# Row maxima of two heads in the two halves of the array, start rows on two queues, routing and experts in an even chain

## The chip, the cores and the metric

The kernel runs on one core of one Trainium2 chip. The metric is the device time of one launch in microseconds (us). Of the kernel before there are three timed runs and one profiled execution.

## What is computed

One transformer layer over 1,024 tokens of width 256, in f32:

```
xn  = layernorm(x)
q, k, v = xn @ Wq.T, xn @ Wk.T, xn @ Wv.T            # 16 heads of 16 columns
scores  = q @ k.T / sqrt(16)                         # causal
std     = softmax(scores) @ v
gsa     = softmax(scores + sensitivity * splat(q, k)) @ v
attn    = ((1 - blend) * std + blend * gsa) @ Wo.T
moe     = two of 16 experts a token (top 2 of sqrt(softplus(xn @ gate.T)) + bias, 128 slots an expert), plus a shared expert
out     = x + attn + moe
```

`splat` is a product of 16 features a head (8 Gaussians, and the same 8 times a tanh) of the query and of the key.

## The kernel before

**Numbers.** The score products run in bf16. Each f32 factor is split in up to three bf16 parts (`split`, line 570 makes the first part, line 575 the second, line 368 on GpSimd and `third_of` on VectorE the third), and six products of parts are stacked along the contraction: `stage` tiles `qs` and `ks` hold for each head 6 x 16 = 96 rows (`RUNS`, `KR`), and two more rows (96 and 97) that subtract the row maximum, which comes as a pair of bf16 rows out of `mT` against rows of ones. `fq` and `fk` hold the same for the features. The rows are copied from `split` by DMA: 12 issues a group of two heads for `qs` and `ks` (`load_qk_row`, line 309), 18 for the features (`load_feature_row`, lines 316 and 322) and one for a correction that is zero here (line 325).

**Groups and slots.** The 16 heads are done two at a time, in 8 groups. A group is 6 pairs of key tiles (`PAIRS`), and a pair has 4 slots, so 24 slots a group. In a pair TensorE runs `std` (scores, line 788, masks line 791), `splat` (line 800, which adds onto the same PSUM banks), and `pv` (line 817: probabilities times v, four streams in the four 32-column strips of the array). ScalarE takes the exponential of each (line 636). Side work goes between them, by a table `PLAN[g][slot]` that all engines walk: on TensorE slot 0 stands between `pv` and the first `splat`, slot 1 between the two `splat`, slot 2 after them, slot 3 between the two `std`. The side work shares three PSUM banks (`AB`); a task waits until the one three places before it has been read (`aux_free`).

**Side work.** `max`/`max2`: the maxima of the next group's rows, plain scores (K = 96, lines 710 to 720) into one bank a head and block, read by VectorE (lines 1088 to 1093), 22 reads a group; `shift`: their transposition and 2 DMAs of 16 rows (line 444); `route` 0 to 7: the top two and the slots, VectorE only but for one product; `sgu`, `shT`, `sy`: the shared expert for one of 8 token tiles; `xT`, `gu`, `hT`, `y`: one of 16 experts (line 735, line 745 with tanh at line 641, line 749, line 754); `oT`, `rows`, `out`: the output; `add`: the gathered expert rows. The shared expert fills groups 0 and 1 (four tiles each), the experts groups 2 to 5 (four each, at slots 0, 2, 5, 6 and 5, 7, 9, 10 of each half group), routing is in slots 1 to 20 of group 0, the adds in groups 6 and 7.

**Before the groups.** `PRO` is the order of TensorE's prologue: transposes of xn, projections, parameters (`par`), features (`feat`, lines 687 to 690), router logits (`gate`, line 669), v (line 695). Then come the maxima of group 0 (`max0`, `PRE1` with 8 of the 16 of `max1`; the other 8 in slots 0 to 3 of group 0), and `std(0,0,0)`, which waits for the shift rows. SyncE issues nearly all transfers, in its program order: after the 24 `qs`/`ks` rows of groups 0 and 1 it reads a flag (`wide`: is a correction needed), branches, issues the 19 feature rows of group 0 with the shift rows among them, and goes on with the table.

Of the kernel before, what the change touches and what calls it, by code (L numbers as in the profile page):

```python
# [6 lines left out]
def bass_splat_attention_moe_layer(nc, x, wqkvo, positions, directions, log_scales, log_amplitudes,  # L7
# [5 lines left out]
    T, D = x.shape  # L13
# [20 lines left out]
    KS = KR + 2  # L34
    NEG = -1.0e30
# [12 lines left out]
    with ctx:  # L48
# [17 lines left out]
        stage = [sb(f"stage{n}", [KS, QB if n < 2 else 2, GH, T], bf16) for n in range(4)]  # L66
# [90 lines left out]
        aux_full, aux_free = sem("aux_full"), sem("aux_free")  # L157
        std_ready, std_exp, gsa_ready, gsa_exp = sem("std_ready"), sem("std_exp"), sem("gsa_ready"), sem("gsa_exp")
# [15 lines left out]
        own_step = sem("own_step")  # L174
# [6 lines left out]
        PRO += [("proj", (s, m, tc)) for m in range(KD) for s in range(2) for tc in range(NC)] + [("par", 0)]  # L181
        PRO += [("feat", (s, tc, w)) for s in range(2) for tc in range(NC) for w in range(2)]
        PRO += [("gate", 0)] + [("v", n) for n in range(NT // 2)]
# [31 lines left out]
        max0 = [("max2", (h,)) for h in range(GH)] + [("max", (h, it, 0)) for h in range(GH) for it in range(2, TC)]  # L215
        max1 = [("max", (h, it, pc)) for h in range(GH) for it in range(TC, NT) for pc in range(2)]
# [12 lines left out]
        SG = 4  # L229
        G0, G1 = 2, 6  # L230
        EG = E // (G1 - G0)


        def spread_late(tasks, first, last):
            late = [n for n in range(first, last + 1) if n % 4]
            return [(late[len(late) * n // len(tasks)], t) for n, t in enumerate(tasks)]
# [6 lines left out]
        def chain(tasks, at):  # L243
            return [(n + 12 * (f // 2), (k, at + f)) for f in range(4) for k, n in tasks[f % 2]]
        SHARED = ((("sgu", 2), ("shT", 5), ("sy", 6)), (("sgu", 7), ("shT", 9), ("sy", 10)))
        EXPERT = ((("xT", 0), ("gu", 2), ("hT", 5), ("y", 6)), (("xT", 5), ("gu", 7), ("hT", 9), ("y", 10)))
        PLAN = []
        for g in range(NG):
            lists = [[(11, ("oT", 0))]]
# [6 lines left out]
            if g == 0:  # L256
                lists.append(spread([("route", k) for k in range(ROUTE)], 1, 22))
            if g < G0:
                lists.append(chain(SHARED, g * SG))
            elif g < G1:  # L260
                lists.append(chain(EXPERT, (g - G0) * EG))
            if g == NG // 2:
                lists.append([(14, ("rows", (0, 0))), (18, ("rows", (0, 1)))])
            if g == NG - 2:
                lists.append(spread([("add", (k, n)) for n in range(TC) for k in range(2)], 12, 22))
            if g == NG - 1:
                lists.append(spread([("add", (k, n)) for n in range(TC, NT) for k in range(2)], 1, 12))
                lists.append([(6, ("out", (TC, 0))), (10, ("out", (TC + 2, 0))), (13, ("rows", (1, 0))),
                              (16, ("out", (0, 2))), (19, ("out", (2, 2)))])
# [21 lines left out]
        def group_of(kind, e):  # L291
            return e // SG if kind in ("sgu", "shT", "sy") else G0 + e // EG

        def count_of(kind, e):
            return place(group_of(kind, e), (kind, e))[1]
# [5 lines left out]
        N_QK, N_F = 12, 19  # L301

        def load_qk_row(eng, g, b, j, done):
            n, h = j // 6, j % 6 // 3
            row, part, num = RUNS[j % 3]
            head = g * GH + h
            m, p0 = head * HD // P, head * HD % P
            src = split[p0:p0 + HD, 0, part:part + 1, m, :].to_broadcast((HD, num, T)) if n == 0 else split[p0:p0 + HD, 1, 0:num, m, :]
            eng.dma_start(stage[n][row:row + num * HD, b, h, :], src).then_inc(done, 16)

        def load_feature_row(eng, g, b, j, done):
# [12 lines left out]
            else:  # L324
                eng.dma_start(fq[KR:KS, b, :, :], gap_d[g:g + 1, :, :, :].rearrange("o s h t -> (o s) h t")).then_inc(done, 16)

        @block.gpsimd
        def _(pool):
# [22 lines left out]
            pool.wait_ge(ones_set, 1)  # L351
# [918 lines left out]
```

## Time and profile before

| | us |
|---|---|
| median of 3 runs | 376.65 (376.22 to 376.99) |
| the profiled execution | 378.75 |
| its span in the trace | 376.9 |
| TensorE matmul busy | 334.7 (89%) |
| VectorE busy | 230.7 (61%) |
| ScalarE busy | 194.1 (51%) |
| GpSimd busy | 65.7 (17%) |
| granted TensorE clock, mean | 0.947 |

Times are us from the span's start. A granted clock of 1.00 is 2.4 GHz, 0.50 is 1.2 GHz. The chain that ended last is 72% TensorE, 14% VectorE, 9% ScalarE. By the first `std` of each group, the groups start at 64.64, 118.37, 155.61, 193.76, 231.92, 270.67, 308.82 and 335.34.

### The profile page before, as it was taken

The page shows a single profiled execution, that of the slowest core. Times are in us where ns is not written, and L with a number is a line of the kernel's source. Part 1 is how long each engine was busy: PE and PEld are TensorE (multiplying, and loading weights), DVE is VectorE, ACT ScalarE, POOL GpSimd, SP SyncE. Part 2 cuts the span into 40 slices and gives each one's busy share as a digit, 9 for nine tenths or more (in the row PEclk, how much of TensorE's full clock was granted, in tenths as well). Part 3 has the DMA queues.
Part 4 walks back from the last instruction along what each step waited for, and adds up shares of the span by engine and source line. Part 5 has one row for each costly group of instructions (what it writes and reads, how often), then busy time and mean ns, then how long its engine had stood idle before and what let it go on. Part 6 is the DMA issues. An engine that isn't in the chain of part 4 may idle for free.

```text
span 376.9 us, 6181 instructions
## 1 busy us (share of the span) xinstructions
PE 334.7 (89%) x2172; PEld 174.8 (46%) x2172; DVE 230.7 (61%) x614; ACT 194.1 (51%) x278; POOL 65.7 (17%) x82
## 2 busy tenths in 40 slices
PE   0999996788979999999999999999999999989965
PEld 0643663343345544554455445544554454335433
DVE  4555857587674665567556655766577558776222
ACT  1699824525414365436543654366346547767530
POOL 7200140400047530110111011102010007710000
PEclk9999768598979999999999999999999999999995
DMA  6408623304341354245655565547555525510011
GB/s 220 131 0 103 107 38 41 60 13 60 47 135 15 41 75 73 71 89 102 142 153 105 113 139 153 107 93 154 129 125 111 79 53 127 143 42 2 0 57 56
DMA packets 27330, 33.01 MB, mean 88 GB/s; under 512 B 6593, under 2 KB 20097, under 8 KB 27297
## 3 DMA queue, kind: packets, MB, share of 16 engines
q1 hardware_dynamic: 23745, 28.32, 37.4%
q0 software_dynamic: 2128, 4.22, 3.9%
q8 instruction: 19, 0.31, 0.4%
q10 hardware_dynamic: 1424, 0.04, 0.2%
q14 instruction: 14, 0.11, 0.1%
HBM read 15.60 MB, written 4.28 MB: 53 GB/s over the span
## 4 chain that ended last, share of the span: by engine, by line
PE 72%; DVE 14%; ACT 9%; issue 3%; DMA 1%; SPq 0%; DVEq 0%; ACTq 0%
PE ps L817 16%; PE ps L745 9%; PE ps L800 8%; PE ps L788 7%; PE ps L754 7%; PE ps L718 6%; ACT arena_p L636 6%; DVE mx L1093 5%; PE ps L676 4%; PE ps L773 2%; PE ps L695 2%; PE ps L758 2%; PE ps L791 2%; DMA acc<-in_x_dram 1%; ACT small L641 1%
## 5 line engine op out<-in xcount | busy, mean ns | idle before, releaser
L636 ACT ACTIVATE arena_p<-ps 128x1024 f32<-128x1024 f32 (+1 forms) x192 | 147.2, 811 | 79.4 <-PE ps L800 53.7
L1093 DVE TENSOR_REDUCE mx<-ps 128x1 f32<-128x512 f32 (+3 forms) x160 | 89.3, 590 | 33.2 <-PE ps L718 22.7
L817 PE MATMUL ps<-arena_p,v_full 128*32 128x512 f32 (+3 forms) x768 | 72.6, 496 | 0.6 <-ACT arena_p L636 0.6
L718 PE MATMUL ps<-stage 96*128 96x512 bf16 (+3 forms) x160 | 51.5, 362 | 7.1 <-DVE mx L1093 4.7
L788 PE MATMUL ps<-stage 98*128 98x512 bf16 (+1 forms) x192 | 51.9, 337 | 4.7 <-ACT arena_p L636 4.2
L800 PE MATMUL ps<-stage 98*128 98x512 bf16 (+1 forms) x192 | 47.4, 332 | 3.0 <-ACT arena_p L636 2.4
L641 ACT ACTIVATE small<-ps 128x176 f32<-128x176 f32 x24 | 7.6, 318 | 64.1 <-PE ps L745 64.1
L387 POOL DMA_INDIRECT wt<-xn_scratch,ids_sb x16 | 15.2, 951 | 133.2 <-PE ps L735 127.6
L817 PEld LDWEIGHTS ps<-arena_p,v_full 128*32 128x32 f32 x768 | 20.2, 110 | 35.4 <-issue 30.3
L754 PE MATMUL ps<-arena_o,small 88*128 88x256 f32 x96 | 27.4, 409 | 8.3 <-DVE small L1116 6.3
L788 PEld LDWEIGHTS ps<-stage 98*128 98x128 bf16 x192 | 18.8, 100 | 23.5 <-ACT arena_p L636 9.8
L718 PEld LDWEIGHTS ps<-stage 96*128 96x128 bf16 x160 | 15.3, 100 | 27.0 <-issue 11.2
L800 PEld LDWEIGHTS ps<-stage 98*128 98x128 bf16 x192 | 14.9, 98 | 26.8 <-ACT arena_p L636 13.5
L791 PE MATMUL ps<-mask_t,ident_b 128*128 128x128 bf16 x128 | 26.5, 225 | 0.0
L754 PEld LDWEIGHTS ps<-arena_o,small 88*128 88x128 f32 x96 | 16.7, 193 | 14.4 <-DVE small L1116 9.7
L745 PE MATMUL ps<-w_sb,wt 128*128 128x352 f32 x64 | 23.0, 482 | 0.1
L395 POOL DMA_INDIRECT ids_scratch<-tok,sidx x16 | 15.5, 968 | 42.0 <-DVE sidx L1047 37.5
L720 PE MATMUL ps<-mask_n,ident_b 128*128 128x128 bf16 x96 | 22.0, 229 | 0.0
L417 POOL DMA_INDIRECT xx<-ye_scratch,gidx x16 | 15.2, 948 | 35.2 <-issue 35.2
L1144 DVE COPY pv_sb<-ps 128x512 f32<-128x512 f32 x16 | 11.1, 692 | 14.6 <-PE ps L817 13.9
L1112 DVE SCALAR_TENSOR_TENSOR small<-small,ps 128x176 f32<-128x176 f32 x24 | 8.1, 338 | 18.1 <-ACT small L641 16.8
L916 DVE TENSOR_TENSOR acc<-ps,acc 128x256 f32<-128x256 f32 (+1 forms) x14 | 7.5, 538 | 18.3 <-PE ps L773 13.5
(193 smaller groups left out, 418.5 us busy)
## 6 DMA issues: line engine op xcount, KB each, us to landing
w_sb<-in_w_dram SPq DMA_DIRECT2D x16, 352.0 KB
stage<-split SPq DMA_DIRECT2D x48, 96.0 KB, 2.9
stage<-split SPq DMA_DIRECT2D x48, 64.0 KB, 2.7
arena_o<-in_w_dram SPq DMA_DIRECT2D x16, 176.0 KB
stage<-split SPq DMA_DIRECT2D x80, 32.0 KB, 2.5
ye_scratch<-wt SPq DMA_DIRECT2D x16, 128.0 KB, 1.8
stage<-split SPq DMA_DIRECT2D x32, 48.0 KB
acc<-in_x_dram SPq DMA_DIRECT2D x2, 512.0 KB, 4.6
```

The lines of the kernel that those rows point to most:

```text
L387: nc.gpsimd.indirect_dma_start(out=xe[:, e % XB, :], out_offset=None, in_=xn_d[:, :], in_offset=bass.IndirectOffsetOnAxis(ap=ids_sb[:, e:e ...
L395: nc.gpsimd.indirect_dma_start(out=ids_d[:, :], out_offset=bass.IndirectOffsetOnAxis(ap=sidx[:, k, n:n + 1], axis=0), in_=tok[:, n:n + 1], ...
L636: A(to, ps[:, 1 + 2 * s:3 + 2 * s, off:CH], ACT.Exp, scale=SCALE).then_inc(done, 1)
L718: ins = M(b[:, 0:n1 - n0], lhs, ks[0:KR, pr, h, n0:n1], start=True, stop=not diag)
L720: ins = M(b[:, n1 - n0 - P:n1 - n0], ident_b[:, :], mask_n[:, :], start=False, stop=True)
L745: ins = M(b[:, 0:2 * I], lhs, w13_sb[:, wb, k, :], start=k == 0, stop=k == KD - 1)
L754: ins = M(b[:, 0:D], hT[:, c, :], w2_sb[:, wb, c, :], start=c == 0, stop=c == 1)
L788: ins = M(b[:, off:CH], ks[:, pr, h, (jb + s) * P:(jb + s + 1) * P], qs[:, pr, h, ic * CH + off:(ic + 1) * CH], start=True, stop=not diag)
L791: ins = M(b[:, off:off + P], ident_b[:, :], mask_t[:, :], start=False, stop=True)
L800: ins = M(ps[:, 1 + 2 * s + h, off:CH], fk[:, pr, h, (jb + s) * P:(jb + s + 1) * P], fq[:, pr, h, ic * CH + off:(ic + 1) * CH], start=Fals ...
L817: ins = M(ps[c:c + 2 * HD, 0, off:CH], v_full[:, jb + s, g * GH + h, :], of, start=jb + s == 0, stop=end)
L1093: V.reduce_max(mx[:, it // TC, h, it % TC, pc:pc + 1], b[:, 0:n1 - n0], AX.X).then_inc(aux_free, 1)
```

## The change

- **Pairs in halves.** The rows of `qs` and `ks` are laid out anew, as four runs a head instead of three: the four largest products of parts fill 64 rows, at partitions 0 to 63 for head 0 and 64 to 127 for head 1; the two others and the shift rows lie in the rest (`QK_RUNS`, `QK_SHIFT`), and head 1's `std` now contracts over 128 rows, of which 30 are zero. The maxima use the 64 rows only (`QK_TOP`): the two heads' matmuls stand next to each other in two halves of the array's rows, then come their two masks over the full array. The two tasks of a pair share a slot, and the first of them waits for both banks. `qs`/`ks` rows are 16 DMAs a group instead of 12; two memsets on GpSimd clear rows 0 to 31 of head 1.
- **Start.** The logits (`gate`) move from after the features to between the projections of the two column halves; the router's exponential, `plus_one` and `softplus` move ahead. GpSimd, not SyncE, reads the flag and branches, after its thirds 6 and 7, and then signals `gaps_ready`, for which SyncE waits ahead of the feature rows of group 0. SyncE issues 12 of these (the query's), then the shift rows; ScalarE issues the 6 of the key. `shift` goes behind the first v on TensorE, not the second. `PRE1` has 4 maxima instead of 8; the other 12 are in slots 0 to 2.
- **Plan.** Routing is spread over slots 8 to 32 (into group 1). The shared expert and the experts are chains: one tile or expert every 4 slots, with the steps of four consecutive experts all in slot 0 of a pair, in the order `y`, `hT`, `gu`, `xT`; shared from slot 8 on, experts from slot 52 (group 2, slot 4) to 124 (group 5, slot 4). The adds are in slots 136 to 180.

```diff
+    QK_RUNS = [[(0, 0, 0, 2), (32, 1, 0, 2), (64, 0, 2, 1), (80, 2, 0, 1)],
+               [(64, 0, 0, 2), (96, 1, 0, 2), (32, 0, 2, 1), (48, 2, 0, 1)]]
+    QK_ALL = [slice(0, KS), slice(0, 128)]
+    QK_TOP = [slice(0, 64), slice(64, 128)]
+    QK_SHIFT = [slice(KR, KS), slice(0, 2)]
...
-        PRO += [("proj", (s, m, tc)) for m in range(KD) for s in range(2) for tc in range(NC)] + [("par", 0)]
+        PRO += [("proj", (s, 0, tc)) for s in range(2) for tc in range(NC)] + [("gate", 0)]
+        PRO += [("proj", (s, 1, tc)) for s in range(2) for tc in range(NC)] + [("par", 0)]
...
+            return [(late[len(late) * (n // GH * GH) // len(tasks)], t) for n, t in enumerate(tasks)]
...
-        LATER = 8
-        first_rest = [(n // 2, ("pre", t)) for n, t in enumerate(max1[LATER:])] + [(4, ("pre", ("shift", 1)))]
+        LATER = 4
+        first_rest = [(n // 4, ("pre", t)) for n, t in enumerate(max1[LATER:])] + [(4, ("pre", ("shift", 1)))]
...
+        def chain(kinds, count, at):
+            return [(at + 4 * (n + step), (kind, n)) for step in range(3, -1, -1) for n in range(count) for kind in kinds[step:step + 1]]
+        S_ROUTE, S_SHARED, S_EXPERT, S_ADD = (8, 32), 8, 52, (136, 180)
+        long = [(at, t) for at, t in chain(("-", "sgu", "shT", "sy"), NT, S_SHARED) if t[0] != "-"]
+        long += chain(("xT", "gu", "hT", "y"), E, S_EXPERT)
+        long += spread([("route", k) for k in range(ROUTE)], *S_ROUTE)
+        long += spread([("add", (k, n)) for n in range(NT) for k in range(2)], *S_ADD)
...
-        N_QK, N_F = 12, 19
+        N_QK, N_F = 16, 19
...
+            for t in (qs, ks):
+                nc.gpsimd.memset(t[0:32, :, 1, :], 0.0).then_inc(rows_clear, 1)
...
+            pool.wait_ge(wide_ready, 1)
+            needed = pool.value_load(wide[0:1, 0:1], min_val=0, max_val=1)
+            for at in POOL_THIRDS[0:2]:
                 third_of(at)
+            with pool.If(needed > 0):
...
+            pool.nop(nofuse=True).then_inc(gaps_ready, 1)
...
             sp.wait_ge(zeros_out, 16)
+            sp.wait_ge(gaps_ready, 1)
             load_feature_row(sp, 0, 0, N_F - 1, f_in[0])
+            for run in range(3):
+                for at in (4, 5):
+                    wait_parts(sp, at, run)
+                for h in range(GH):
+                    for w in range(2):
+                        load_feature_row(sp, 0, 0, 6 * h + 2 * run + w, f_in[0])
             shift_rows(-1, 0, 0)
...
+            def maxima_of_heads(g, t, pr):
+                kind, a = t
+                places = [place(g, (kind, (h,) + a[1:])) for h in range(GH)]
+                if places[1][1] > AB:
+                    pe.wait_ge(aux_free, places[1][1] - AB)
+                blocks = [(0, 0, P, 0), (1, 0, 2 * P, P)] if kind == "max2" else [(a[1], a[2] * CH, min((a[1] + 1) * P, (a[2] + 1) * CH), 0)]
+                for it, n0, n1, at in blocks:
+                    diag, last = n1 == (it + 1) * P, it == blocks[-1][0]
+                    for h in range(GH):
+                        rows, b = QK_TOP[h], ps[:, places[h][0], :]
+                        ins = M(b[:, at:at + n1 - n0], qs[rows, pr, h, it * P:(it + 1) * P], ks[rows, pr, h, n0:n1],
+                                start=True, stop=not diag)
+                        if last and not diag:
+                            ins.then_inc(aux_full, 1)
+                    for h in range(GH if diag else 0):
+                        end = at + n1 - n0
+                        ins = M(ps[:, places[h][0], end - P:end], ident_b[:, :], mask_n[:, :], start=False, stop=True)
+                        if last:
+                            ins.then_inc(aux_full, 1)
```

## Rows read from the trace of the kernel before

**Rows 1.** The table of stretches: start:end, length, busy of PE, PEld, DVE, ACT, POOL, granted clock, DMA share, GB/s.

```profile
64.64:81.38 16.74, 13.68 (x76) 6.88 (x75) 12.54 (x39) 7.31 (x12) 4.20 (x2) 0.72 0.25 39
81.38:118.37 36.99, 31.45 (x180) 15.08 (x180) 24.53 (x81) 13.60 (x19) 7.82 (x8) 0.86 0.35 65
118.37:155.61 37.24, 35.46 (x252) 18.22 (x250) 22.69 (x59) 19.27 (x28) 10.86 (x11) 1.00 0.36 51
155.61:193.76 38.15, 36.64 (x260) 19.14 (x259) 24.12 (x63) 19.39 (x28) 3.79 (x4) 1.00 0.55 124
107.96:114.90 6.94, 6.94 (x23) 3.93 (x27) 3.97 (x11) 0.90 (x3) 5.03 (x6) 0.51 0.59 170
```

**Rows 2.** The table of lines by form: line, engine, operation, count, busy, mean ns, idle before.

```profile
L636 ACT ACTIVATE arena_p<-ps 128x1024 f32<-128x1024 f32 x96 | 95.1, 1025 | 52.8 <-PE ps L800 29.2 <-PE ps L788 12.8 <-PE ps L791 10.3
L1093 DVE TENSOR_REDUCE mx<-ps 128x1 f32<-128x512 f32 x96 | 65.3, 686 | 28.3 <-PE ps L718 22.7 <-PE ps L720 4.7
L718 PE MATMUL ps<-stage 96*128 96x512 bf16 x96 | 38.3, 403 | 5.6 <-DVE mx L1093 3.7 <-DVE mx L1089 1.5
L745 PE MATMUL ps<-w_sb,wt 128*128 128x352 f32 x64 | 23.0, 482 | 0.1
```

**Rows 3.** Timeline of PE in group 3: start, length, line, tile, count.

```profile
208.35 0.60 PE L800 MATMUL ps<-stage 98*128 98x512 bf16 x2
208.88 0.22 PE L723 MATMUL ps<-ident_b,mhl 128*16 128x128 bf16 x1
209.04 0.50 PE L718 MATMUL ps<-stage 96*128 96x512 bf16 x2
...
213.74 1.92 PE L817 MATMUL ps<-arena_p,v_full 128*32 128x512 f32 x16
215.60 0.44 PE L735 MATMUL ps<-ident,wt 128*128 128x128 f32 x2
...
231.92 0.38 PE L788 MATMUL ps<-stage 98*128 98x512 bf16 x1
232.14 0.22 PE L791 MATMUL ps<-mask_t,ident_b 128*128 128x128 bf16 x1
232.20 0.38 PE L788 MATMUL ps<-stage 98*128 98x512 bf16 x1
```

**Rows 4.** Timeline of PE, start and group 0; in brackets the idle time before and its releaser.

```profile
40.38 4.47 PE L669 MATMUL ps<-gw_sb,xx 128*128 128x16 f32 x32
...
64.64 0.63 PE L788 MATMUL ps<-stage 98*128 98x512 bf16 x1
...
69.50 1.01 PE L800 MATMUL ps<-stage 98*128 98x512 bf16 x2 [2.09 <-ACT arena_p L636]
...
89.52 1.10 PE L754 MATMUL ps<-arena_o,small 88*128 88x256 f32 x4 [1.75 <-DVE small L1116]
...
107.96 1.95 PE L754 MATMUL ps<-arena_o,small 88*128 88x256 f32 x4 [2.17 <-DVE small L1116]
```

**Rows 5.** Timeline of ACT at the start.

```profile
35.34 0.69 ACT L556 ACTIVATE arena_o<-ps,par 128x512 f32<-128x512 f32 x1 [0.17 <-PE ps L690]
...
47.08 1.06 ACT L575 ACTIVATE split<-arena_p 128x1024 bf16<-128x1024 f32 x1 [1.08 <-DVE arena_p L923]
```

**Rows 6.** Timeline of POOL at the start: thirds 6 and 7.

```profile
46.15 4.96 POOL L368 TENSOR_TENSOR split<-arena_p,split 128x1024 bf16<-128x1024 f32 x2 [31.47 <-ACT split L575]
```

**Rows 7.** Timeline of SP's issues (SPq) at the start: each length is issue time.

```profile
27.15 16.15 SPq L309 DMA_DIRECT2D stage<-split  x24
43.35 0.58 SPq L453 DMA_DIRECT2D w_sb<-in_ws_dram  x1
47.71 0.31 SPq L325 DMA_DIRECT2D stage<-gap_scratch  x1
48.14 9.29 SPq L316 DMA_DIRECT2D stage<-split  x12
57.47 1.35 SPq L444 DMA_DIRECT2D stage<-mT  x2
```

More of the change, by code:

```diff
@@ L64, in bass_splat_attention_moe_layer @@
         v_full = sb("v_full", [P, NT, H, 2 * HD], f32)
-        stage = [sb(f"stage{n}", [KS, QB if n < 2 else 2, GH, T], bf16) for n in range(4)]
+        stage = [sb(f"stage{n}", [P, QB, GH, T] if n < 2 else [KS, 2, GH, T], bf16) for n in range(4)]
         qs, ks, fq, fk = stage
@@ L214, in bass_splat_attention_moe_layer @@
         NSLOT = 4 * NP
[L215 to L216 removed]
+        max0 = [("max2", (h,)) for h in range(GH)] + [("max", (h, it, 0)) for it in range(2, TC) for h in range(GH)]
+        max1 = [("max", (h, it, pc)) for it in range(TC, NT) for pc in range(2) for h in range(GH)]
         def spread(tasks, first, last):
@@ L299, in shape_of @@
             return off, jb // TC == ic
-        N_QK, N_F = 12, 19
+        N_QK, N_F = 16, 19
+        ROWS_QK = [(n, h) + run for n in range(2) for h in range(GH) for run in QK_RUNS[h]]
         def load_qk_row(eng, g, b, j, done):
-            n, h = j // 6, j % 6 // 3
-            row, part, num = RUNS[j % 3]
+            n, h, row, part, first, num = ROWS_QK[j]
             head = g * GH + h
             m, p0 = head * HD // P, head * HD % P
-            src = split[p0:p0 + HD, 0, part:part + 1, m, :].to_broadcast((HD, num, T)) if n == 0 else split[p0:p0 + HD, 1, 0:num, m, :]
+            src = split[p0:p0 + HD, 0, part:part + 1, m, :].to_broadcast((HD, num, T)) if n == 0 else split[p0:p0 + HD, 1, first:first + num, m, :]
             eng.dma_start(stage[n][row:row + num * HD, b, h, :], src).then_inc(done, 16)
@@ L614, in _, with key_feature_rows @@
             part1(7)
-            act.wait_ge(gate_dve, 1)
-            A(g_[2][:, :, :], g_[1][:, :, :], ACT.Exp, scale=-1.0).then_inc(gate_act, 1)
-            for n in range(NT // 2):
-                evacuate(("v", n))
+            def key_feature_rows(run):
+                for at in (6, 7):
+                    wait_parts(act, at, 2 - run)
+                for h in range(GH):
+                    load_feature_row(act, 0, 0, 12 + 3 * h + run, f_in[0])
+            key_feature_rows(2)
+            key_feature_rows(1)
+            evacuate(("v", 0))
+            key_feature_rows(0)
+            evacuate(("v", 1))
             act.wait_ge(gate_dve, 2)
             A(g_[4][:, :, :], g_[3][:, :, :], ACT.Ln).then_inc(gate_act, 1)
+            evacuate(("v", 2))
+            evacuate(("v", 3))
             act.wait_ge(gate_dve, 3)
@@ L701, in aux @@
                 if kind == "add" or (kind == "route" and a != CUM):
+                    return
+                if kind in ("max2", "max"):
+                    if a[0] == 0:
+                        maxima_of_heads(g, t, pr)
                     return
@@ L787, in std @@
                     b = ps[:, 1 + 2 * s + h, :]
-                    ins = M(b[:, off:CH], ks[:, pr, h, (jb + s) * P:(jb + s + 1) * P],
-                            qs[:, pr, h, ic * CH + off:(ic + 1) * CH], start=True, stop=not diag)
+                    rows = QK_ALL[h]
+                    ins = M(b[:, off:CH], ks[rows, pr, h, (jb + s) * P:(jb + s + 1) * P],
+                            qs[rows, pr, h, ic * CH + off:(ic + 1) * CH], start=True, stop=not diag)
                     if diag:
@@ L858, in _ @@
             prologue(n_v)
-            prologue(n_v + 1)
             aux(-1, ("shift", 0), 0)
-            prologue(n_v + 2)
-            prologue(n_v + 3)
+            for n in range(1, NT // 2):
+                prologue(n_v + n)
             for t in PRE1:
```

165 lines of the change are left out of this document (68 added, 97 removed).

## The prediction, made before the kernel was run

> **What bounds the kernel now.** I read the table of stretches first, cut at the first `std` of each group. From group 1 on TensorE sets the pace: in groups 1 and 2 it is busy 35.46 of 37.24 us and 36.64 of 38.15 at a clock of 1.00, while VectorE has 23 to 24 us of work and ScalarE 19 [rows 1]; groups 3 to 5 repeat group 2 (38.2 to 38.8 us). There a gain has to come out of TensorE's own stream or out of its 1.5 us of idle time a group. Group 0 is another matter: with 53.7 us (16.74 + 36.99) it is 16 us longer than the next, at clocks of 0.72 and 0.86, and VectorE is as loaded as TensorE [rows 1]. Then I read the timelines. In group 0 TensorE waits 1.75 and 2.17 us for the evacuation of `shT` (a copy that stands behind routing and maxima on VectorE), and right behind the second wait it runs 6.94 us at a clock of 0.51 [rows 4, 1]. Before the groups, `std(0,0,0)` starts at 64.64 and the first `splat` at 69.50, and the queue of SyncE issues feature and shift rows nearly without a pause from 47.71 on [rows 4, 7].
>
> **1. Pairs in halves.** In a stream of one array shape a 512-column bf16 matmul holds TensorE for 0.22 us (231.92 to 232.14) and a mask of 128 columns for 0.06 [rows 3]; the mean of 403 ns of the maxima [rows 2] is a duration with its latency and not the price. A head has 4,608 columns of maxima a group, nine times 512, so 1.94 us; if the two heads run at once a group saves 1.94 us. That streams in parts of the array do run at once the trace shows for strips: `pv` puts 16 f32 pieces of 512 columns through in 1.86 us (213.74 to 215.60), under 0.12 each, where even a bf16 piece of 512 columns alone takes 0.22 [rows 3]. Against it stands the change of shape. The 16-column transpose starts at 208.88, where the two matmuls before it ended their columns at 208.35 + 2 x 0.22 = 208.79, and after its own 0.06 the next starts at 209.04: 0.10 us on either side [rows 3]. A pair of maxima enters the halves and leaves them, 11 pair tasks a group, `max2` twice: 24 changes a group. For halves of the rows the trace shows no case. The bounds are 0 (from 98 to 128 active rows there is no gap, 231.92 to 232.14) and 0.10 (the strips); I take 0.08, nearest to the strips. Then 24 x 0.08 = 1.92 us go for 1.94 gained: **0 a group**, from -1.94 (no gap) to +0.46 (0.10), so over 8 groups from -15.5 to +3.7.
> The Trainium skill, page TensorEngine Tiling (Array Packing), section Key Properties, says that tiles work independently but that changing the tiling mode, not just the tile, drains the engine. By it the end with no gap falls away and the pairs are worth about nothing or a little less; no row here shows it for halves of the rows.
> Head 1's `std` over 128 rows instead of 98 costs nothing (98 and 128 active rows run at the same pace [rows 3]). The 4 more DMAs a group are 4 x 0.67 = 2.7 us of issue on SyncE (24 in 16.15 [rows 7]); SyncE is not what TensorE waits for in a group, but it counts at the start.
>
> **2. The start.** `gate` is 32 small matmuls in 4.47 us [rows 4]. Its work was behind the features, beside ScalarE's and VectorE's splitting; now it stands in front of the second half of the projections, and all that follows in that chain is late by it. Nothing covers it: at 35.34 ScalarE was already waiting for TensorE's features [rows 5], and from there it works without a gap to the last second part at 47.08. So that ends at 48.14 + 4.4 = 52.5, and GpSimd's third 7, which ended at 51.1 [rows 6], ends at 55.5. Before, SyncE read the flag itself, from 43.93 to 47.71, 3.8 us, hidden beside the last splits of the query features [rows 7]. Now it waits for GpSimd's branch behind the third: 0 to 3.8 us for it, I take 1.5: 57.0. The 32 `qs`/`ks` rows (32 x 0.67 = 21.5) and the weights are issued by 49.3, so SyncE idles. Then the gap row 0.4, 12 feature rows 9.3 and the shift rows 1.35 [rows 7] end at 68.1; before, the shift rows were out by 58.8 and the last feature rows, now on idle ScalarE, at 65.5. With about 1.8 us to landing `std(0,0,0)` starts near 69.9 instead of 64.64. The first `splat`, which waited for a late square root and exponential on ScalarE until 69.50 [rows 4], comes one `std` (1.1) and one exponential (1.03 [rows 2]) later, at 72.2: +2.7. The twelve maxima left for slots 0 to 2 are 7.4 us of VectorE work behind that instead of 5.5: **+3.0 us** at slot 8 (from 0, if the flag's branch is free and the rows overlap, to +5).
> The two memsets on GpSimd delay the ones and xn's copy by some 5 us; xn's copy was ready 13 us before its reader. Nothing.
>
> **3. The rest of group 0.** It took 36.99 us with 31.45 us of TensorE at a clock of 0.86 [rows 1], so 27.0 at full clock. One `sgu`, two `shT` and three `sy` leave it for groups 1 and 2: 1.2 + 0.4 + 2.6 = 4.2 us, which leaves 22.8. VectorE's 24.53 [rows 1] loses 2.8 for these and 5.9 of routing, and gets 8.6 of routing (steps 0 to 5): 24.4. `sy` and `shT` now wait for a copy made four slots earlier, so the waits of 1.75 and 2.17 go [rows 4], and with them likely the low clock behind them (6.94 us at 0.51 [rows 1], of which half is lost, and 1.7 us lost after the other). What is late next is VectorE, in whose order routing and maxima stand. The stretch lies between 25 and 33 us; I take 29: **-8.0 us**. The 4.2 us come back in groups 1 and 2, where TensorE is full: **+4.2**.
>
> **4. The chains of experts.** TensorE's work is the same, only denser: one expert (about 2.5 us) a pair instead of two thirds. What changes are the waits. Taken away: `y` behind its own `hT`, part of the 1.5 us idle a group; over groups 1 to 5 I take -3.5 of 7.5. Added: tanh now stands on ScalarE between the two `std` exponentials and waits for `gu`, which comes late in slot 0; behind it stand the second `std` exponential and both of `splat`. From the end of `gu` to the end of that exponential are 0.15 + 0.32 + 1.03 = 1.5 us, and TensorE has `xT` 0.2, one `splat` 0.43 and a pair of maxima 0.45 to fill it: 0.4 us are open where all columns are full, less than nothing in the pairs on the diagonal. Two of six pairs are full, 24 pairs carry a chain: 8 x 0.4 = 3.2; but TensorE's queue of maxima fills some: **+2**. Bounds: 0 and 24 x 0.45 = +10.8. In sum **-1.5**. Maxima come two at a time (2 x 0.69 us of VectorE [rows 2]) with three banks; that is within the bound. The adds were not waited for: 0.
>
> **Sum.** 0 + 3.0 - 8.0 + 4.2 - 1.5 = -2.3 us. On the profiled execution's 378.75 that is 376.4; it lies 2.1 us above the median of the runs, so against 376.65: **374.4 us**. A change within 0.2% (0.75 us) can't be told from none here.
>
> **Rivals.** *A: the halves change without a gap.* For it: active rows change freely; against it: every change of columns shows 0.10 us [rows 3]. It gives up to -15.5; the groups would then stand at 34 to 36 us and ScalarE's and VectorE's waits take a few back: about 361 us.
> *B (slower): the dense slot.* `y`, `hT`, `gu`, `xT` in one slot make ScalarE's tanh and VectorE's four copies late for what TensorE wants next. It decides from the point where the open 0.45 us appears in most of the 24 pairs instead of the 8 full ones, because maxima wait for two free banks and no longer fill the gap: +10.8 instead of +2, so 374.4 + 8.8 = 383. For it: VectorE has two maxima (1.4 us), four evacuations (2.0) and at times `oT` in one pair of 7 us; against it: two of three pairs have short columns.
> *C: group 0 doesn't shorten*, because VectorE's 24.4 us are in line with TensorE at every step and the clock stays low: 34 us instead of 29, and 374.4 + 5 = 379.5.
> *D: expert weights come late.* They are asked for after `y` and wanted one pair later, 13 or more slots before; DMA share 0.55 [rows 1] becomes about 0.75. If each of 13 waits 0.8 us: 385.
>
> **Chances.** My case 0.36 (own range 370 to 379; about three quarters of it faster, one tenth within 0.2%), A 0.20 (faster), B 0.28, C 0.12 and D 0.04 (slower, but for a few parts in a hundred that a smaller form of B or C ends near or below the time before). Together faster 0.51, within 0.2% 0.10, slower 0.39. The range for 8 in 10 leaves out the deep end of A and the far end of B and D: 362 to 384.
>
> **What would show it.** Pairs: the time between the end of the columns before a pair and its first matmul, and behind it, 0.08 on each side, and the two heads' matmuls starting within 0.02 us of each other; if they start 0.22 apart the halves don't run at once. Start: GpSimd's third 7 ends at 55.5, SyncE's gap row near 57, shift rows near 67, `std(0,0,0)` near 69.9, first `splat` near 72. Group 0: no wait of over 1 us ahead of `sy`, from slot 8 to group 1 about 29 us at a clock above 0.95. Groups 3 and 4 with six and five experts near 43 us, group 6 unchanged near 26.5. I am wrong if the groups without experts become shorter by over 1 us (A), if ScalarE's second `std` exponential is waited for in most pairs (B), or if `std(0,0,0)` starts before 66.

## The result, and the profile after

The changed kernel takes 410.60 us (median of 4 runs) against 376.82 for the kernel before on the same chip: 1.0895 times as long, with a 95% interval of 1.0846 to 1.0943. That is +33.8 us where I forecast -2.3. The profiled execution has a span of 408.2 us; TensorE is busy 81% of it, before 89%.

The stretches of the changed kernel, cut at the first `std` of each group (columns as in [rows 1]):

```profile
72.59:123.34 50.75, 40.12 (x234) 15.47 (x238) 31.18 (x83) 18.95 (x27) 2.51 (x2) 0.80 0.22 36
123.34:166.48 43.14, 38.68 (x263) 19.37 (x267) 29.29 (x94) 19.25 (x30) 18.68 (x19) 1.00 0.38 69
166.48:206.03 39.55, 34.99 (x251) 16.98 (x255) 23.27 (x61) 19.40 (x29) 4.56 (x5) 1.00 0.40 87
206.03:255.10 49.07, 42.45 (x279) 22.22 (x283) 27.41 (x74) 19.70 (x31) 5.67 (x7) 0.97 0.52 132
255.10:303.37 48.27, 41.62 (x285) 22.22 (x289) 28.53 (x76) 19.74 (x31) 3.03 (x4) 1.00 0.51 128
303.37:333.36 29.99, 27.15 (x217) 11.83 (x221) 19.30 (x50) 18.63 (x25) 12.87 (x14) 1.00 0.48 108
333.36:366.67 33.31, 26.68 (x207) 10.89 (x211) 20.80 (x52) 18.69 (x25) 2.37 (x3) 0.95 0.28 50
```

In group 2 before, TensorE was idle for 1.5 of 38.15 us [rows 1]. Here every stretch from group 1 on has 2.8 to 6.7 us of idle time (first number less PE's busy time). Against before, the first `std` is 8.0 us later, group 0 is 3.0 shorter (50.75 for 53.73), and groups 1 to 6 together are 26.4 longer.

The costliest groups of instructions name the new idle time: 41.7 us stand ahead of the paired maxima (L744). VectorE's reads of maxima ended 17.7 us of it (L1133, the line below) and 5.9 us more (L1129, the reads of `max2`), its second operation on `gu` 5.4 us, its copy of `mT` 3.9 us. Before, TensorE stood idle for 5.6 us ahead of the maxima of 512 columns [rows 2].

```profile
L744 PE MATMUL ps<-stage 64*128 64x512 bf16 (+2 forms) x192 | 34.2, 347 | 41.7 <-DVE mx L1133 17.7
```

Timeline of TensorE in group 3, and of VectorE beside it:

```profile
221.08 0.38 PE L846 MATMUL ps<-stage 98*128 98x256 bf16 x2
222.33 0.39 PE L744 MATMUL ps<-stage 64*128 64x512 bf16 x2 [0.87 <-DVE small L1153]
222.66 0.29 PE L750 MATMUL ps<-mask_n,ident_b 128*128 128x128 bf16 x2
...
223.76 0.39 PE L744 MATMUL ps<-stage 64*128 64x512 bf16 x2 [0.49 <-DVE mx L1133]
```

```profile
221.85 0.34 DVE L1153 SCALAR_TENSOR_TENSOR small<-small,ps 128x176 f32<-128x176 f32 x1
222.11 0.42 DVE L1149 COPY wt<-ps 128x256 f32<-128x256 f32 x1
222.93 1.29 DVE L1133 TENSOR_REDUCE mx<-ps 128x1 f32<-128x512 f32 x2 [0.40 <-PE ps L750]
...
224.74 1.28 DVE L1133 TENSOR_REDUCE mx<-ps 128x1 f32<-128x512 f32 x2
```

The halves do run at once: two matmuls of 512 columns end within 0.39 us of their common start, where two in one shape need 0.60 [rows 3]; in the trace their two records start 6 ns apart (222.334 and 222.340 us). But the pair at 222.33 has waited until VectorE's second operation on the bank of `gu` was over at 222.19, and the next pair (223.76) until the first of the two reads, which take 1.29 us together, had cleared a bank at 223.62. There are three banks, and a pair takes two.

### The profile page after: what moved, and what is told of

Its sections match the earlier page's. It is cut to its first block, busy times and chain, and to the rows that moved or that the text cites. A ratio compares the mean times of both kernels' runs of the same rounds, so it can differ in the third digit from the quotient of the medians.

```text
span 408.2 us, 6196 instructions
## 1 busy us (share of the span) xinstructions
PE 332.1 (81%) x2148; PEld 163.4 (40%) x2172; DVE 231.7 (57%) x614; ACT 194.2 (48%) x278; POOL 71.4 (17%) x84
## 4 chain that ended last, share of the span: by engine, by line
PE 64%; DVE 16%; ACT 8%; SPq 5%; issue 4%; DMA 2%; DVEq 0%; another core or an unknown queue 0%
PE ps L863 16%; PE ps L790 7%; PE ps L744 7%; PE ps L799 6%; DVE mx L1133 6%; PE ps L834 5%; ACT arena_p L670 4%; PE ps L710 4%; PE ps L846 3%; PE ps L750 3%; PE ps L729 2%; SPq L312 2%; PE ps L818 2%; PE ps L837 2%; ACT small L675 2%
## 5 line engine op out<-in xcount | busy, mean ns | idle before, releaser
L1133 DVE TENSOR_REDUCE mx<-ps 128x1 f32<-128x512 f32 (+3 forms) x160 | 87.8, 591 | 30.0 <-PE ps L744 18.0
L863 PE MATMUL ps<-arena_p,v_full 128*32 128x512 f32 (+3 forms) x768 | 77.0, 521 | 1.0 <-ACT arena_p L670 0.6
L744 PE MATMUL ps<-stage 64*128 64x512 bf16 (+2 forms) x192 | 34.2, 347 | 41.7 <-DVE mx L1133 17.7
L834 PE MATMUL ps<-stage 98*128 98x512 bf16 (+5 forms) x168 | 46.4, 332 | 8.8 <-ACT arena_p L670 5.1
L846 PE MATMUL ps<-stage 98*128 98x512 bf16 (+1 forms) x192 | 46.6, 332 | 5.1 <-ACT arena_p L670 5.0
L744 PEld LDWEIGHTS ps<-stage 64*128 64x128 bf16 x192 | 11.0, 93 | 72.4 <-issue 58.4
L834 PEld LDWEIGHTS ps<-stage 98*128 98x128 bf16 x192 | 17.5, 101 | 22.1 <-issue 13.7
L846 PEld LDWEIGHTS ps<-stage 98*128 98x128 bf16 x192 | 15.1, 99 | 24.0 <-issue 11.1
L790 PE MATMUL ps<-w_sb,wt 128*128 128x352 f32 x64 | 21.7, 461 | 0.0
L1160 DVE COPY wt<-ps 128x256 f32<-128x256 f32 x16 | 6.8, 425 | 22.1 <-PE ps L799 22.1
```

The source lines that it names most:

```text
L744: ins = M(b[:, at:at + n1 - n0], qs[rows, pr, h, it * P:(it + 1) * P], ks[rows, pr, h, n0:n1], start=True, stop=not diag)
L790: ins = M(b[:, 0:2 * I], lhs, w13_sb[:, wb, k, :], start=k == 0, stop=k == KD - 1)
L834: ins = M(b[:, off:CH], ks[rows, pr, h, (jb + s) * P:(jb + s + 1) * P], qs[rows, pr, h, ic * CH + off:(ic + 1) * CH], start=True, stop=not ...
L846: ins = M(ps[:, 1 + 2 * s + h, off:CH], fk[:, pr, h, (jb + s) * P:(jb + s + 1) * P], fq[:, pr, h, ic * CH + off:(ic + 1) * CH], start=Fals ...
L863: ins = M(ps[c:c + 2 * HD, 0, off:CH], v_full[:, jb + s, g * GH + h, :], of, start=jb + s == 0, stop=end)
L1133: V.reduce_max(mx[:, it // TC, h, it % TC, pc:pc + 1], b[:, 0:n1 - n0], AX.X).then_inc(aux_free, 1)
```

## The experiments

There are eighteen runs of sixteen kernels; `start_plus_one` repeats the start alone, `route_again` repeats `route_only`. Each stands against runs of the kernel before on its own chip; on one of the chips that kernel takes 411 us instead of 377, so for the runs there only ratios and steady groups are compared.

**The three parts alone.** The edits are those of the change, sorted.

> Of the change only the pairs: rows of the two heads in the halves, 16 row transfers a group, both heads' maxima issued together in one slot; the start and the plan of the experts as before. Theory 1 (a pair waits for two of three banks at once, and VectorE has them): slower by 10 to 25 us against before, with idle time ahead of the pairs' matmuls of over 15 us, also in groups 4 to 6, where no expert's work runs in the changed kernel. Theory 2 (the dense slots of the new plan cost, the pairs by themselves are free): within 2 us of before. Theory 3 (the start costs most): within 2 us of before as well.

> Only the plan: routing over slots 8 to 32, the shared and the experts' steps all in slots with s = 0, two adds a slot from 136; the maxima one head a slot as before, the start as before. Theory 1: within 3 us of before. Theory 2 (four steps of different experts in one slot keep ScalarE and VectorE late): slower by 10 to 20 us. My prediction had the two chains at +4.2 - 1.5 and group 0 at -8, so about -5.

> Only the start: gate early, third 7 on POOL behind the gap row's wait, rows over three queues, shift next to its maxima, 4 instead of 8 maxima of the second half left out of group 0's list. Theory 3 says it costs what the changed kernel's first std shows, +7 to +8 us at the first std, less what group 0 gives back: +3 to +8 in all. Theories 1 and 2: at most +3.

> Pairs and plan, the start as before. If the costs add up, this is the sum of the two single runs. Theory of the interplay (a pair in slot 1 waits for the bank that gu of slot 0 holds until ScalarE and VectorE are done with it): over 5 us more than the sum of the single runs, and VectorE's reads of gu among what ends the idle time ahead of the pairs. With the start it makes the changed kernel's +34 us, so I expect +24 to +32 here.

> The changed kernel without its pairs: plan and start only. If the parts add up, +2 and +11 us, so 389 to 391, and the pairs take the other 20 to 22 us of the changed kernel's +34.

```
kernel              us       ratio to before (95% interval)
pairs             402.16     1.0664 (1.0608 to 1.0720)
plan              379.02     1.0032 (1.0004 to 1.0060)
start             387.88     1.0299 (1.0251 to 1.0347)
pairs and plan    402.63     1.0693 (1.0638 to 1.0748)
plan and start    387.07     1.0182 (1.0129 to 1.0235)
all three         410.60     1.0895 (1.0846 to 1.0943)
```

The pairs cost 6.6% alone, 6.6% on top of the plan (1.0693 / 1.0032) and 7.0% on top of plan and start (1.0895 / 1.0182): 25 us, whatever stands around them. So theory 2 falls, and the interplay with the dense slot, which would have put the two over 5 us above their sum, isn't there either. The start alone costs more than the 3 to 8 us that I had written down for it. Start and plan share something: 1.2 and 11.3 us by their ratios, but 6.9 together, where I had expected 389 to 391 us (2 and 11 more); what they share I did not look for. The price of the pairs alone lies in all groups that run maxima: +2.6 us in group 0, +4.1, +4.0, +3.4, +4.7 and +2.4 in groups 1 to 5, +1.5 in group 6.

**Pairing without halves, halves without pairing.**

```
bunch:         pairs as in the change, but   rows = slice(0, KR)   for both heads
halves_apart:  rows = QK_TOP[h], each head in its own slot and in the old order
```

> The kernel before with one edit: the maxima of both heads stand in one slot and are issued one behind the other (the pair's wait for both banks included), but with all 96 rows and the layout and the 12 row transfers of before, so no halves. Theory 1 (the two reductions, 1.29 us on VectorE, and the wait for two of three banks are the cost): +14 to +24 us, idle time of TensorE in the third group up from 1.5 to over 4 us. Rival (the halves cost: change of shape, 16 transfers): within 4 us of before.

> The opposite edit: halves' layout with its 16 row transfers a group, but each head's maximum alone in its own slot, in the order of before. Nothing is overlapped, and each of the 28 matmuls of a group that read 64 rows is entered and left with a change of shape. At the 0.10 us against 0.02 that the changed kernel shows at either side this is 28 x 2 x 0.08 = 4.5 us a group, +31 us over seven; if only every other change costs, +16. The waits for VectorE should be near those of before (1.5 us idle a group) by theory 1; if the rows' layout or transfers cause the waits, they are 4 us here too.

Measured: `bunch` 1.0437 (1.0388 to 1.0487), +16.5 us, with runs spread from 390.16 to 396.85 us; `halves_apart` 1.0516 (1.0447 to 1.0586), +19.5 us, nearer to the 16 of my second case than to the 31 of the first. Both are dear, and for different reasons, as the third group (first `std` of group 3 to that of group 4) shows in the tables of stretches of pairs alone, of `bunch` and of `halves_apart`:

```profile
204.65:246.18 41.53, 36.81 (x259) 17.62 (x258) 24.15 (x63) 19.43 (x28) 3.79 (x4) 1.00 0.51 117
```

```profile
197.04:237.43 40.39, 36.37 (x260) 19.00 (x258) 24.21 (x63) 19.42 (x28) 3.78 (x4) 1.00 0.55 120
```

```profile
202.12:242.57 40.45, 39.35 (x259) 18.48 (x258) 24.52 (x63) 19.42 (x28) 3.78 (x4) 1.00 0.52 118
```

The like group before has 38.15 us, 36.64 of them busy [rows 1]. `halves_apart` has its 2.3 us more as busy time and waits no longer than before (1.1 us idle): that is the change of shape. A single matmul of 64 rows is entered and left with 0.10 us each (the next start comes 0.31 to 0.32 us later instead of 0.22), and nothing is won, since nothing runs beside it. `bunch` has no change of shape; its 2.2 us more are idle time, 4.0 us in all. The pairs have both: 0.4 us more busy than `bunch` and 4.7 us idle. So the halves as such don't pay even for their changes of shape, and putting two maxima in one slot, in alternating order of the heads, costs 2.5 us of idle time a group.

**Is it VectorE's reading time?** One edit in each, on the pairs and on the kernel before:

```
- V.reduce_max(..., b[:, 0:n1 - n0], AX.X)
+ V.reduce_max(..., b[:, 0:P], AX.X)
```

> The pairs alone, but VectorE reads only the first 128 columns of each maximum (0.29 us instead of 0.69 at 512 columns); part of the maximum is left out, TensorE's work is unchanged. Theory 1 (the pair waits for VectorE to clear two banks): the idle time of the third group falls from 4.7 to 2 us or less and 2.5 to 3.5 us a group come back, 15 to 22 us in all: 380 to 387. Rival (TensorE pays for the halves itself: shape changes, transfers): at most 5 us back.

> The control: the kernel before with the same short reads. Its third group idles 1.5 us, so at most 1 us a group can come back: 0 to 8 us faster by every theory. The price of the pairs with VectorE out of the way is the difference between this and the run above: within 5 us by theory 1, near 20 us by the rival.

Measured: 384.49 and 363.33 us; the kernel before was 377.41. Short reads give the pairs 4.7% back (from 1.0664 to 1.0164, 384.5 us, inside theory 1's 380 to 387), but the control gains 3.8% itself (0.9621), 14.1 us where I had written at most 8. The difference between the two, the price of the pairs with VectorE nearly out of the way, is 21.2 us: by the numbers written down, the rival's. But the traces don't show its mechanism, that TensorE pays for the halves itself. In the third group the control has 36.60 us (35.72 busy) and the pairs with short reads 39.06 (36.31 busy): 1.9 of the 2.5 us between them are again idle. The idle time of that group falls from 4.7 to 2.75 us, where theory 1 asked for 2 or less. Added up over groups 2 to 5, TensorE's waits of 0.1 us and more are 1.1 us a group before, 3.7 in `bunch`, 4.1 in the pairs, 0.6 and 2.3 in the two kernels with short reads. The largest one of the pairs is `y` waiting for the copy of its `hT`: 1.08 us a group against 0.28. Here is what stands ahead of that copy (L1145) in VectorE's queue in the pairs alone, and what TensorE does meanwhile:

```profile
215.81 1.29 DVE L1122 TENSOR_REDUCE mx<-ps 128x1 f32<-128x512 f32 x2 [1.67 <-PE ps L732]
217.13 0.17 DVE L1127 TENSOR_SCALAR mneg<-mx 128x8 f32<-128x8 f32 x1
217.34 0.17 DVE L1131 CAST mhl<-mneg 128x8 bf16<-128x8 f32 x1
217.54 0.17 DVE L945 TENSOR_TENSOR mhl<-mneg,mhl 128x8 bf16<-128x8 f32 x1
217.63 0.41 DVE L1145 COPY small<-ps 88x256 f32<-88x256 f32 x1
```

```profile
215.66 0.38 PE L776 MATMUL ps<-ident,small 128*88 128x128 f32 x2
216.55 0.44 PE L762 MATMUL ps<-ident,wt 128*128 128x128 f32 x2 [0.51 <-DVE mx L1122]
216.83 0.28 PE L828 MATMUL ps<-stage 98*128 98x128 bf16 x2
218.19 1.10 PE L781 MATMUL ps<-arena_o,small 88*128 88x256 f32 x4 [1.08 <-DVE small L1145]
```

The same place in the kernel before, TensorE's timeline, and then VectorE's, where the copy is L1116:

```profile
202.50 0.38 PE L749 MATMUL ps<-ident,small 128*88 128x128 f32 x2
202.72 0.38 PE L735 MATMUL ps<-ident,wt 128*128 128x128 f32 x2
202.94 0.28 PE L800 MATMUL ps<-stage 98*128 98x128 bf16 x2
203.41 0.38 PE L718 MATMUL ps<-stage 96*128 96x512 bf16 x1 [0.19 <-DVE mx L1093]
203.62 0.22 PE L720 MATMUL ps<-mask_n,ident_b 128*128 128x128 bf16 x1
203.74 1.10 PE L754 MATMUL ps<-arena_o,small 88*128 88x256 f32 x4
```

```profile
202.70 0.56 DVE L1093 TENSOR_REDUCE mx<-ps 128x1 f32<-128x384 f32 x1 [0.81 <-PE ps L720]
203.18 0.41 DVE L1116 COPY small<-ps 88x256 f32<-88x256 f32 x1
203.51 0.41 DVE L1109 COPY wt<-ps 128x256 f32<-128x256 f32 x1
203.88 0.69 DVE L1093 TENSOR_REDUCE mx<-ps 128x1 f32<-128x512 f32 x1
```

Before, one read of 0.56 us stands ahead of the copy; the last maximum of the half (TensorE at 203.41, its read at 203.88) comes behind it, and TensorE has that maximum to do until the copy lands. With the pairs both reads and, because they complete the half, the three small operations of the shift stand ahead of it, and TensorE's slot has no maximum left to fill the time. Short reads take 0.4 us off that wait and leave 0.68. `xT`'s transpose at 216.55 waits for one of the two banks, 0.94 us a group, of which short reads leave 0.11. No run gave the side work a fourth bank, and none let the first head start when its own bank is free, so how much of the price is the banks and how much the order in VectorE's queue isn't shown.

**Other slots for the pairs.**

```
FREE0, FREE1 = (1, 3, 4), (7, 8, 11, 13, 15, 16, 19, 20)
maxima = [(FREE0[n // GH], t) for n, t in enumerate(max0)] + [(9, ("shift", 0))]
maxima += [(FREE1[n // GH], t) for n, t in enumerate(max1)] + [(22, ("shift", 1))]
```

> The pairs alone, in groups 1 to 5 moved to slots in which mostly no shared or expert's step stands (1, 3, 4 and 7, 8, 11, 13, 15, 16, 19, 20 instead of 1, 2, 5 and 7, 9, 10, 11, 14, 15, 17, 18). Theory 1b (the price is the meeting of a pair's two reads with an expert's step in VectorE's queue and in the three banks): idle time of groups 2 to 5 from 4.1 to 2.3 us a group or less, 7 to 12 us back, 390 to 395. Rival 1c (a pair makes slots of uneven length wherever it stands, and the short ones don't cover ScalarE's exponentials): idle 3.5 to 5 us, at most 4 us back.

> Both heads in one slot with all 96 rows, in the same slots as the run above. Theory 1b: groups 2 to 5 at 38 to 39 us, within 8 us of before. Rival 1c: groups at 40 us as in the run bunch, 13 to 17 us slower. The difference between this run and the one above is the price of the halves themselves: 24 changes of shape a group at 0.10 us less 1.94 saved, +0.5 a group, 3 to 4 us.

Measured: `pairs_free` 1.0763 (1.0693 to 1.0834) and `bunch_free` 1.0561 (1.0513 to 1.0608): no better than in the old slots. The waits of groups 2 to 5 are 4.7 and 4.2 us a group. My placement made a new one, 1.67 us ahead of the second shift, because its last pair stands at slot 20; without it 3.0 and 2.5 us are left, so avoiding the experts' steps takes away 1.1 to 1.2 us a group and no more. The wait of 1.08 us for the copy of `hT` is there again to the digit, with the same five operations ahead of it on VectorE: the pair now at slot 4 completes the half. That is between the two theories in idle time, and by the times on the side of 1c. Which slots would make pairs cheap stays open. By the medians of these two runs the halves cost 9.5 us, where I expected 3 to 4; pairs alone less `bunch` is 8.7. Part of that is the clock. In the profiled executions the pairs alone spend 52.3 us at a granted clock of 0.50, most of it in stretches that begin behind a wait, `bunch` 38.4, before 42.3; half of the 13.9 us between the first two, 7 us, is lost. But the profiled execution of `bunch` (390.16 us, clock 0.955) was its fastest. By span times (1 - granted clock) of every run, the pairs lose 25 us and `bunch` 17 to 24, so the clock is about 3 of the 8.7 us at the medians. The changes of shape are some 3 us (0.4 a group), and the 4 more row transfers a group account for 0.4 us of waits a group.

**The start.**

```
start_late_plus:  plus_one()  from behind rest_of(2) to behind rest_of(7)
start_fixed:      plus_one()  to behind aux(-1, ("shift", 0)); gaps_ready raised before
                  GpSimd's first two thirds instead of behind them
```

> The start alone once more, one look, as the partner of the next two: first std at 73, +11 us in all.

> The start alone, with the gate's six VectorE instructions behind the exponential (plus_one) moved from ahead of the third rest to behind the eighth. Theory 3a (VectorE stands from 35.8 to 38.7 behind the exponential, then the third rest starts at 41.6 instead of 32.2 and takes the whole chain of ScalarE and POOL along): the last product of ScalarE back from 54.0 to about 48 to 50, the gap row from 57.9 to 52 to 54, first std back by 3.5 to 6 us, time +5 to +7 us instead of +11. Rival 3b (the gate ahead on TensorE and the rows' new order cost): at most 1.5 us back.

> The start alone, with plus_one moved behind the first shift and the gap row let go before POOL's two thirds. Left of the start's price: the gate's matmuls ahead of the second half of the projections on TensorE (3.9 us later there). Theory 3a: first std at 67 to 70 instead of 73.1, +3 to +6 us on before. Rival 3b: first std above 71, +9 us.

`start_plus_one` is the start alone once more: first `std` at 72.5, 389.55 us, 11.4 above before. Timeline of VectorE in the first run of this kernel (first `std` at 72.9), and then of ScalarE:

```profile
39.05 0.23 DVE L1025 TENSOR_SCALAR w_sb<-w_sb 128x128 f32<-128x128 f32 x1 [3.27 <-ACT w_sb L618]
...
41.62 1.22 DVE L947 SCALAR_TENSOR_TENSOR rest<-xx,split 128x1024 f32<-128x1024 f32 x1
```

```profile
38.73 0.30 ACT L618 ACTIVATE w_sb<-w_sb 128x128 f32<-128x128 f32 x1
...
42.88 1.06 ACT L588 ACTIVATE split<-rest 128x1024 bf16<-128x1024 f32 x1 [2.41 <-DVE rest L947]
```

VectorE waits 3.27 us for the gate's exponential, does 2.6 us of gate work, and only then the rest on which ScalarE waits 2.41 us. I had not priced that. `start_late_plus` takes the wait away; ScalarE's last second part starts at 51.0 instead of 54.0 and the gap row goes out at 55.0 instead of 57.9. Yet only 0.5% comes back, 1.0245 (1.0218 to 1.0272), because the six operations meet another thing. VectorE and GpSimd:

```profile
50.89 2.14 DVE L1025 TENSOR_SCALAR w_sb<-w_sb 128x128 f32<-128x128 f32 x1
53.07 2.04 DVE L1027 TENSOR_SCALAR w_sb<-w_sb 128x128 f32<-128x128 f32 x1
55.15 0.23 DVE L1028 TENSOR_SCALAR w_sb<-w_sb 128x128 f32<-128x128 f32 x1
```

```profile
50.08 4.95 POOL L376 TENSOR_TENSOR split<-arena_p,split 128x1024 bf16<-128x1024 f32 x2 [35.76 <-ACT split L588]
```

An operation of 0.23 us takes 2.14 and 2.04, each until one of GpSimd's two is over (at 52.96 and 55.03). With 1.90 us more of idle time ahead of them, for which no releaser is shown, the maxima start at 59.1 instead of 53.9. The Trainium skill, page SBUF — State Buffer, section SBUF: two separate sides, says that GpSimd and VectorE, when VectorE's operation is in a 2-port mode or has two SBUF inputs, share one pair of ports as an exclusive lock: whoever starts first has it for the whole instruction, and the other waits. The trace agrees as far as it goes (2.14 and 2.04 us, each ending 0.07 to 0.08 us behind GpSimd's); in which mode these operations run it doesn't show.

`start_fixed` gives nearly all back: 1.0035 (0.9992 to 1.0077), first `std` at 64.2 instead of 72.9, where I had written 67 to 70. Theory 3a explains only a part of it. In the start alone the first `std` waits 6.70 us for the shift rows, which SyncE issues from 70.42 on, behind the gap row (57.86) and twelve feature rows; in `start_fixed` the gap row goes out at 43.85 and the shift rows at 57.34. The exponential alone (`start_late_plus`) brought the first `std` forward by 1.3 us only. The early gap row wasn't run alone, so the two shares stay open. What is left of the start (early gate, new row order, 4 deferred maxima) costs at most 0.8% on that chip.

**The part that helps.**

```
- if g == 0: lists.append(spread([("route", k) for k in range(ROUTE)], 1, 22))
+ route = spread([("route", k) for k in range(ROUTE)], 8, 32)
+ lists.append([(at - g * NSLOT, t) for at, t in route if at // NSLOT == g])
```

> The kernel before with one part of the plan: the eight routing steps over slots 8 to 32 instead of 1 to 22; shared and experts' steps as before. Theory (group 0's surplus is VectorE's gate and routing work beside the maxima, and the clock that falls while TensorE waits for it): group 0 down from 53.5 to 46 to 50 us, group 1 up by at most 1.5, 3 to 6 us faster than before. Rival (group 0 got shorter in the plan run because two of its four shared tokens' steps moved to group 1): within 1.5 us of before.

> The kernel before with the routing over slots 8 to 32 (3.3 us faster than before by itself) and 4 instead of 8 of the first maxima ahead of the first slot. If group 0 now has room on VectorE, the first std comes 2 to 4 us earlier and group 0 takes 0 to 3 us more: 370 to 374. Else group 0 grows by all of it or more: 374 to 378.

> The routing spread alone once more, in more rounds: 0.988 to 0.994 of before as in the first run, if that wasn't the chip. On a chip on which TensorE stands while the sixteen indirect transfers of the routing run, the gain may be gone, since they start 10 us later.

> The routing spread together with the start as mended (plus_one behind the first shift, the gap row let go early, 4 maxima ahead of the first slot). If the parts add up (0.991 times 1.0035), 0.994 to 0.996 of before; better than the routing spread alone only if the four maxima that move into group 0 find room there, 0.985 to 0.990.

`route_only` is faster than both kernels: 373.57 us, 0.9913 (0.9884 to 0.9943), 3.3 us. Group 0 goes from 53.7 to 49.0 us, group 1 from 37.2 to 38.2, the time at the low clock from 42.3 to 28.8 us. By span times (1 - granted clock) of every run, the low clock costs 14 us here at the median and 17 in the kernel before, which is about the whole gain. The other three ran on the chip with the slow kernel before: `route_later4` 1.0059 (1.0031 to 1.0086), `route_again` 1.0027 (0.9995 to 1.0059), `route_start` 1.0029 (0.9996 to 1.0062). There the gain is gone, as I had allowed for in `route_again`; `route_later4` and `route_start` miss what I had written down (370 to 378 us, and 0.985 to 0.996). Group 0 has its 49.3 us there too, but group 1, beside which the routing's indirect transfers now run, has 56.7; I didn't profile the kernel before on that chip, so whether the later start of these transfers eats the gain is open. `route_later4` shows that the first `std` can come at 59.8, but group 0 then takes 57.1 us. A gain on one chip and none on the other is what can be claimed.

## Why the prediction was wrong

**1. Pairs: 0 predicted, +25.2 us measured; this is the step that failed.** What I worked out came true. The two heads start together, and the change of shape takes 0.10 us on either side where I took 0.08; with 24 x 0.10 = 2.4 us for 1.94 gained, 0.5 us a group, TensorE's stream fits the 0.4 us that the pairs are busier than `bunch`, inside my bounds. What failed is that TensorE's own stream was the whole sum. The waits of the pair were one clause in step 4 ("Maxima come two at a time (2 x 0.69 us of VectorE) with three banks; that is within the bound"), and the bound was that of another mechanism. In groups 2 to 5 TensorE's waits are 3 us a group longer than before (4.1 for 1.1), and group 6, which has no expert's work, is 1.5 us longer too. `bunch`, which has the pairing without the halves, costs 16.5 of the 25.2 us; the halves on top cost 8.7, more than their changes of shape, and that rest is only in part explained. The trace of before had the means to price them: VectorE's two reads and the shift's operations in line, 1.3 + 0.5 us, ahead of the copy on which `y` waits, and the next slot without a maximum.

**2. Start: +3.0 predicted, +10.9 us measured alone.** The events that I listed came in the right order but later: GpSimd's third 7 ended at 60.0 (55.5), the gap row was issued at 59.8 (57), the shift rows at 71.4 (67), the first `std` at 72.6 (69.9), the first `splat` at 75.4 (72.2). The flag's branch cost nothing. Two terms were missing or mis-sized. One is the exponential on whose result VectorE's queue stands still, ahead of the third rest. I had written that ScalarE works without a gap up to 47.08, but the line shows it waiting 1.08 us there for VectorE [rows 5], so that chain ran through VectorE, too. The other is the gap row behind GpSimd's two thirds: with it SyncE's whole row of transfers starts late, and I charged the first `splat` 2.7 us for it, 0.2 more than my own terms add up to (69.9 + 1.1 + 1.03 = 72.0). `start_fixed`, which mends both, is 0.35% above before, so together they were the price. In the changed kernel:

```profile
55.08 4.96 POOL L380 TENSOR_TENSOR split<-arena_p,split 128x1024 bf16<-128x1024 f32 x2 [38.08 <-ACT split L596]
```

```profile
59.84 0.27 SPq L328 DMA_DIRECT2D stage<-gap_scratch  x1
60.21 9.78 SPq L319 DMA_DIRECT2D stage<-split  x12
70.04 1.34 SPq L485 DMA_DIRECT2D stage<-mT  x2
```

**3. Group 0: -8.0 predicted, right for the plan alone** (53.7 to 45.2 us). VectorE was not as loaded as TensorE there, as I had read it: 37.1 us against 45.1 over the group [rows 1]. `route_only` gives 4.7 us of it, with the routing spread alone. With all three parts group 0 is 50.75 us: on top of plan and start (44.7 us) the pairs take 6 us there too.

**4. Chains: 4.2 - 1.5 = +2.7 predicted for groups 1 to 6, +9.3 in the plan alone.** Groups 3 and 4, for which I had said near 43, are 45.3 and 45.7 us: the added waits are mis-sized, inside the bounds of step 4. Group 6, "unchanged near 26.5", is 28.1 with the plan and 33.3 with all. Of the latter, 2.68 us are a wait for rows that SyncE issued late (its 16 end at 336.2), and a stretch of 3.4 us at a clock of 0.50 follows it.

```profile
338.55 0.23 PE L744 MATMUL ps<-stage 64*128 64x128 bf16 x2 [2.68 <-DMA stage<-split]
...
340.60:344.00 3.40, 3.40 (x22) 2.12 (x26) 2.59 (x8) 0.99 (x3) 0.00 (x0) 0.50 0.37 48
```

Rival C (its sum is 379.4, not 379.5) has the changed kernel's group 0, 3.0 us shorter than before, but not for its reason: the plan alone takes 8.5 us off it, and the pairs put 6 back. Rival B had the slower side and part of the place: it said that maxima wait for two free banks, but only as a reason why the dense slot's gap isn't filled, 0.45 us in 24 pairs. The runs show two maxima in one slot, with the waits that follow, as the main cost, and the dense slots as the smaller one (6.6 us more than forecast in groups 1 to 6). The range ended at 384, its far end from B and D; neither held a price for the pairs in groups without experts (+2.6, +4.1 and +1.5 us in groups 0, 1 and 6).

## What to carry to other kernels

Where an in-order engine empties what TensorE fills, price a batched step on both sides: what stands ahead of each copy in the reader's queue, and which banks are left, before counting columns. Take the work that fills a wait as a resource: here a maximum of its own slot (203.41) covered the wait for a copy, and once both maxima stood in one slot that wait was open. A wait put early in an engine's order (here for an exponential) costs what stands behind it in that order, so follow it to the next engine that starves.

## What the runs showed of the hardware

- VectorE's TENSOR_SCALAR of 128x128 took 2.14 and 2.04 us beside GpSimd's TENSOR_TENSOR, 0.23 alone (`start_late_plus`).
- A change between 64 and more rows costs 0.10 us each way (`halves_apart`), as between 128 and 16 columns [rows 3]. Not every change of columns does: in the kernel before, a transpose of 88 columns (L749) starts 0.06 us behind a mask of the full array (209.435 and 209.375), which is the mask's own time; rival A's "every change of columns" went too far. The Trainium skill, page TensorEngine Tiling (Array Packing), section Key Properties, says that a change of mode drains TensorE; the trace agrees for 64 rows, 0.31 to 0.32 us between starts instead of 0.22.
- On the slower chip TensorE stands still for 6 to 15 us at a time while GpSimd issues its two series of sixteen indirect transfers (7.8 and 9.2 us in `start_fixed`, 8.8 and 6.4 in `route_again`, 15.0 and 6.4 in `route_start`). In `route_start`, where I looked at all engines in the second stop, VectorE and ScalarE stop with it, and no work of this core is named as what releases them. Its timeline, all engines:

```profile
330.91 0.22 PE L748 MATMUL ps<-mask_n,ident_b 128*128 128x128 bf16 x1
...
334.02 0.94 POOL L453 DMA_INDIRECT xx<-ye_scratch,gidx  x1 [0.30 <-issue]
...
336.76 0.60 ACT L664 ACTIVATE arena_p<-ps 128x512 f32<-128x512 f32 x1 [7.06 <-remote]
336.81 0.56 DVE L1114 TENSOR_REDUCE mx<-ps 128x1 f32<-128x384 f32 x1 [6.86 <-remote]
...
337.51 0.59 PE L816 MATMUL ps<-stage 98*128 98x512 bf16 x1 [6.38 <-issue]
```

What holds them is open. The other chips show no such stop, and the steady groups are the same on both (38.16 us).
